# Moving one subtraction on the Vector engine: the low half of a head's first probability unit goes from ahead of row 7's maximum to behind the next head's first maxima

## The chip, the core and the metric

The kernel runs on one core of one Trainium2 chip. The metric is the device time of one execution in microseconds (us), lower is better. The engines are named as the profile names them: PE is TensorE (matmuls), DVE is VectorE, ACT is ScalarE, POOL is GpSimd, and SP is the engine whose queue issues the DMAs.

## The reference

A block of a transformer on x of shape 4 x 1024 x 512, in float32:

```
xn  = layernorm(x)
q, k, v = xn @ Wq.T, xn @ Wk.T, xn @ Wv.T          # 16 heads of 32 columns
scores  = q k^T / sqrt(32), causal mask
attn    = softmax(scores) @ v  -> @ Wo.T
gate    = silu((xn @ fp8(gate_w)) * gate_scale)
up      = (xn @ fp8(up_w)) * up_scale
ffn     = ((gate * up) @ fp8(down_w)) * down_scale   # inner width 1536
out     = x + attn + ffn
```

With 4 batches and 16 heads there are 64 attention heads of 1024 x 1024 scores each, and the feed-forward part works on 4096 rows.

## The kernel before

A first stage (up to about 285 us) normalises x, projects q, k and v, and prepares weights. Then `attend` runs 16 iterations of four heads (s = 0, 1, 2, 3; head n = 4 it + s). Each head is cut into nine steps (u = 0 to 8), so an iteration has 36 steps (k = 9 s + u). Between the attention work of the steps PE gets matmuls of the feed-forward part and, from iteration 4 on (`with_out`), of the output projection. Nothing is scheduled at run time: each engine has its own program, written out step by step with tables such as `LOW_STEP`, executes it in order, and waits on semaphores where it needs another's result.

A head's probabilities are made in two ways. The first six rows of 128 queries are made transposed, in six units of up to 512 columns: PE writes the scores of unit u (`scores`, L1453), ACT takes the exponential into one of five buffers p32 (`exponentials`, L1269), POOL zeroes the masked triangle (`select`, L1206), ACT copies the float16 high half (`take_high`, L1259), and DVE or POOL subtracts it to get the low half (`take_low`, L1060). DVE makes the low halves of units 0, 3 and 5, POOL those of 1, 2 and 4. Rows 6 and 7 of 128 queries are made untransposed: PE writes their scores into a pair of banks (`scores_of_row`, L1467, ending with the mask, L1471), DVE takes their maximum and turns it into a bias (`maximum_of_row`, L1395 and L1398), ACT takes the exponential (`exponentials_of_row`, L1276) and the high half (L1283), POOL the low half (`low_of_row`, L1212), and a transposing DMA (L1096) turns them for PE. The scores of unit 3 on PE wait until row 7's exponential has read its banks.

For the head two further on, PE and DVE find the maxima of the first six rows ahead of time: PE writes scores (`maxima_scores`, L209) into two banks in turn, DVE reduces them (`row_maxima`, L232, each followed by the read of its accumulator, or L237), eight such units numbered 0 to 7 in steps 4 to 8, and PE can fill a bank only when DVE has reduced the maxima two units earlier. PE turns the maxima of head n+1 (L262), DVE copies them (`copy_row`, L269), and SP stores them as a row into that head's q_st (`store_row`, L199), without which PE can't begin that head (L1453).

Further steps of DVE that matter here: `normalise` (L1352, L1353, L1358) ends a half of the head before; L1358 multiplies two SBUF tiles. `swiglu` (L1383, L1390) multiplies gate and up. In s = 0 and 1, `scale_down` (L1376) frees bank `misc` at u = 5; in s = 2 and 3, from iteration 4 on, `add_output` (L1367) frees it at u = 4 (k = 22 and 31). PE's turning of the maxima waits for whichever it is. On SP, in s = 3, the store of the output that L1367 makes (L1138) and a load of 512 KB of x (L1118) stand ahead of the next head's row (L199), and behind it the two transposes of the rows (L1096) and then the load of the next iteration's xn tile (L1084), which PE's first gate matmul (L1515) needs. POOL also makes the low halves of the fused feed-forward tile (L1194) and of the attention output (L1190), and adds the feed-forward result to x (L1186).

The order of DVE's steps within a head comes from `iteration` in the DVE block, L1401 to L1423:

```
if u == 4 and n > 0: normalise(n - 1, 0)
swiglu ...
if u in ROW_MAX_STEP: maximum_of_row(...)            # row 6 at u = 1, row 7 at u = 3
row_maxima(..., n + 2, ..., M_STEP.get(u, ()))       # u = 4: maxima units 0 and 1
for unit, head in of_head(LOW_STEP, n, u): take_low(...)
copy_row; normalise(n - 1, 1) at u = 8; add_output; scale_down
```

`LOW_STEP = {2: 0, 3: 1, 4: 2, 8: 3, 9: 4, 10: 5}` gives the step of each unit; 10 is step 1 of the next head. POOL uses the same table for its units.

Of the kernel before, what the change touches and what calls it, by code (L numbers as in the profile page):

```python
# [113 lines left out]

E_STEP = {0: 0, 1: 1, 2: 2, 6: 3, 7: 4, 8: 5}
HIGH_STEP = {1: 0, 2: 1, 3: 2, 7: 3, 8: 4, 9: 5}
LOW_STEP = {2: 0, 3: 1, 4: 2, 8: 3, 9: 4, 10: 5}
ROW_SCORES_STEP = {1: 0, 3: 1}
ROW_MAX_STEP = {1: 0, 3: 1}
# [44 lines left out]
def of_head(table, n, u):  # L164


    found = [(table[u], n)] if u in table else []
    if u + U in table and n > 0:
        found.append((table[u + U], n - 1))
    return found  # L170
# [787 lines left out]
def attend(nc, x, out, xn_dram, keep, rows, pair, bank):  # L958
# [5 lines left out]
    with ExitStack() as ctx:  # L964
# [88 lines left out]
        def take_low(eng, ops, units, u, n, signal):  # L1053

            if u not in units:
                return
            e, at = NE * n + u, slice(u * 512, u * 512 + UNIT_WIDTH[u])

            eng.wait_ge(p_hi, e + 1)
            ops.tensor_tensor(probs[n % 2][:, LO, at], p32[e % RING][:, 0:UNIT_WIDTH[u]], probs[n % 2][:, HI, at],  # L1060
                              ALU.subtract).then_inc(signal, 1)
# [111 lines left out]
        def _(pool):  # L1173
# [23 lines left out]
            def select(u, n):  # L1197

                if u not in DIAGONAL:
                    return  # L1200
                pool.wait_ge(exp_done, NE * n + u + 1)
                blocks = 2 if DIAGONAL[u] else 1
                step = DIAGONAL[u] or P
                at = p32[(NE * n + u) % RING][:, :].rearrange("p (b q) -> p b q", q=P)
                at = at[:, 0:(blocks - 1) * (step // P) + 1:step // P, :]
                nc.gpsimd.affine_select(out=at, in_=at, compare_op=ALU.is_ge, fill=0.0, base=0,  # L1206
                                        pattern=[[0, blocks], [1, P]], channel_multiplier=-1).then_inc(diag_done, 1)
# [7 lines left out]
            def iteration(it, with_out):  # L1215
                for s in range(HEADS_PER_IT):
                    n = 4 * it + s
                    for u in range(U):
                        k = s * U + u
                        if u in E_STEP:  # L1220
                            select(E_STEP[u], n)
                        for unit, head in of_head(LOW_STEP, n, u):
                            take_low(pool, nc.gpsimd, POOL_LOW, unit, head, p_lo_pool)
# [24 lines left out]
        def _(act):  # L1248
            def take_high(u, n):

                e, w = NE * n + u, UNIT_WIDTH[u]
                act.wait_ge(exp_done, e + 1)
                if u in DIAGONAL:

                    act.wait_ge(diag_done, ND * n + sorted(DIAGONAL).index(u) + 1)
                if u == 0:

                    wait(act, pv_mm, 2 * (n - 1))
                nc.scalar.copy(probs[n % 2][:, HI, u * 512:u * 512 + w], p32[e % RING][:, 0:w]).then_inc(p_hi, 1)  # L1259

            def exponentials(u, n):

                e, w = NE * n + u, UNIT_WIDTH[u]
                act.wait_ge(e_mm, e + 1)

                old = e - RING
                wait(act, p_lo_pool, low_parts(POOL_LOW, old))
                wait(act, p_lo_dve, low_parts(DVE_LOW, old))
                nc.scalar.activation(p32[e % RING][:, 0:w], st_bank[u % 2][:, 0:w],  # L1269
                                     ACT.Exp, scale=s_exp[:, :]).then_inc(exp_done, 1)  # L1270
# [29 lines left out]
            def iteration(it, with_out):  # L1300
                for s in range(HEADS_PER_IT):
                    n = HEADS_PER_IT * it + s
                    for u in range(U):
                        k = s * U + u
                        if u in E_STEP:
                            exponentials(E_STEP[u], n)
                        for unit, head in of_head(HIGH_STEP, n, u):
                            take_high(unit, head)
# [38 lines left out]
        def _(dve):  # L1347
# [53 lines left out]
            def iteration(it, with_out):  # L1401
                for s in range(HEADS_PER_IT):
                    n = 4 * it + s
                    for u in range(U):
                        k = s * U + u
                        if u == 4 and n > 0:
                            normalise(n - 1, 0)
                        for f, t in at_step(SWIGLU_STEP, it, k):
                            swiglu(f, t)
                        if u in ROW_MAX_STEP:  # L1410
                            maximum_of_row(ROW_MAX_STEP[u], n)
                        if n + 2 < NH:
                            row_maxima(nc, dve, rows, m_bank, n + 2, s % 2, M_STEP.get(u, ()))
                        for unit, head in of_head(LOW_STEP, n, u):
                            take_low(dve, nc.vector, DVE_LOW, unit, head, p_lo_dve)
                        if k in ROW_STEP and n + 1 < NH:
                            copy_row(nc, dve, rows, misc, n + 1, (s + 1) % 4, it if s == 0 else it + 1)
                        if u == U - 1 and n > 0:
                            normalise(n - 1, 1)
                        if with_out and k in ADD_OUT_STEP:  # L1420
                            add_output(ADD_OUT_STEP[k], it - LAG)
                        if k in ADD_DOWN_STEP and it > 0:
                            scale_down(ADD_DOWN_STEP[k], it - 1)  # L1423
# [271 lines left out]
```

## Time and profile before

| | before |
|---|---|
| median of 3 runs | 1320.91 us (1313.93 to 1323.89) |
| the profiled execution | 1318.2 us, of it span 1316.5 us |
| PE busy | 1240.5 us (94%) |
| DVE busy | 1074.4 us (82%) |
| ACT, POOL busy | 897.8 us (68%), 876.9 us (67%) |
| mean granted TensorE clock | 0.992 |
| DVE L1060 (low halves) | 192 instructions, 113.7 us, mean 605 ns |
| POOL L1212 (low halves of rows) | 128 instructions, mean 2017 ns |

Share of busy time alone does not say what bounds the kernel: PE's matmuls are pipelined and their ends are modelled, and the engines hand work to each other several times in each step. A wait is booked in brackets ahead of the instruction that waited ("[0.66 <-PE pair L1471]": the engine stood idle 0.66 us until PE's line 1471 wrote the pair of banks). An instruction of DVE or POOL can also be held up after it has started; then it has no bracket, and its own duration is longer than that of its equals.

### The profile page before, as it was taken

The numbers are of one execution on the slowest core, as the hardware profiler recorded it, in microseconds if no ns is written. First come the engines' busy times: TensorE is split into PE (matmuls) and PEld (weight loads), VectorE is DVE, ScalarE is ACT, GpSimd is POOL, SyncE is SP. The second block draws the span as 40 slices with busy tenths as digits, with TensorE's granted clock in tenths as the row PEclk, the third lists the DMA queues.
The fourth block names the chain that finished last, engine by engine and source line by source line (L and its number), as shares of the span: only waits on it lengthen the run. The fifth ranks groups of instructions, "written<-read, shape, count | busy, mean of one in ns | idle before, by whom it ended". The sixth has DMA issues, their size and how long they took to land.

```text
span 1316.5 us, 32425 instructions
## 1 busy us (share of the span) xinstructions
PE 1240.5 (94%) x11749; PEld 819.5 (62%) x11749; DVE 1074.4 (82%) x2615; ACT 897.8 (68%) x1527; POOL 876.9 (67%) x1017
## 2 busy tenths in 40 slices
PE   4999999987899898999999999999999999999988
PEld 3444444446666666677776767676767676776654
DVE  8888788868888888887988888888878787878862
ACT  4323323237777878788888888787878787878870
POOL 1332233127777777788887887877878787888882
PEclk9999999989999999999999999999999999999999
DMA  8699999834546464666666675767666556667555
GB/s 267 167 248 242 262 267 236 212 111 93 131 100 141 99 136 94 129 128 137 146 130 150 117 150 102 150 122 151 128 140 121 138 122 138 142 127 150 103 110 119
DMA packets 427599, 196.07 MB, mean 149 GB/s; under 512 B 339248, under 2 KB 396592, under 8 KB 427440
## 3 DMA queue, kind: packets, MB, share of 16 engines
q1 hardware_dynamic: 409024, 177.22, 60.4%
q10 hardware_dynamic: 18416, 16.78, 4.7%
q8 instruction: 94, 1.54, 0.5%
q14 instruction: 65, 0.53, 0.1%
HBM read 72.89 MB, written 42.21 MB: 87 GB/s over the span
## 4 chain that ended last, share of the span: by engine, by line
PE 45%; DVE 14%; issue 5%; DMA 5%; ACT 4%; POOL 3%; SPq 2%; ACTq 0%; DVEq 0%; POOLq 0%
PE bank L1515 14%; PE bank L1529 10%; PE bank L1491 7%; PE pair L1453 4%; PE pair L209 4%; DVE probs L1060 3%; DMA shared<-xn_parts 3%; PE bank L1537 2%; DVE row_top L1395 2%; DMA q_st<-m_row 2%; PE pair L1467 2%; DVE junk L232 2%; ACT probs L1259 2%; POOL row L1212 2%; DVE ga L1383 2%
## 5 line engine op out<-in xcount | busy, mean ns | idle before, releaser
L1269 ACT ACTIVATE p<-pair,s_exp 128x512 f32<-128x512 f32 (+1 forms) x384 | 243.6, 635 | 171.5 <-PE pair L1453 170.2
L1212 POOL TENSOR_TENSOR row<-row 128x896 f16<-128x896 f32 (+1 forms) x128 | 257.2, 2017 | 12.1 <-ACT row L1283 12.0
L1060 POOL TENSOR_TENSOR probs<-p,probs 128x512 f16<-128x512 f32 x192 | 223.0, 1165 | 0.2
L1259 ACT CAST probs<-p 128x512 f16<-128x512 f32 (+1 forms) x384 | 214.4, 558 | 10.8 <-POOL p L1206 9.0
L1515 PE MATMUL bank<-shared,wg 128*128 128x256 f16 x1536 | 201.9, 275 | 3.5 <-DMA shared<-xn_parts 3.5
L1515 PE MATMUL bank<-shared,wu 128*128 128x256 f16 x1536 | 202.4, 275 | 0.0
L1529 PE MATMUL bank<-wd,fuse 128*128 128x512 f16 x768 | 192.3, 381 | 0.8 <-DVE ff_out L1376 0.8
L1395 DVE TENSOR_REDUCE row_top<-pair 128x1 f32<-128x896 f32 (+1 forms) x128 | 147.6, 1153 | 44.3 <-PE pair L1471 44.3
L1206 POOL TENSOR_SCALAR_AFFINE_SELECT p<-p 128x128 f32<-128x128 f32 (+1 forms) x256 | 104.0, 411 | 118.2 <-ACT p L1269 117.6
L1194 POOL TENSOR_TENSOR fuse<-fu,fuse 128x512 f16<-128x512 f32 x96 | 120.7, 1257 | 62.5 <-ACT fuse L1298 62.3
L1515 PEld LDWEIGHTS bank<-shared,wg 128*128 128x128 f16 x1536 | 142.5, 98 | 29.7 <-DMA shared<-xn_parts 8.0
L1515 PEld LDWEIGHTS bank<-shared,wu 128*128 128x128 f16 x1536 | 143.6, 99 | 22.1 <-issue 0.2
L1276 ACT ACTIVATE row<-pair,row_bias,s_exp 128x896 f32<-128x896 f32 (+1 forms) x128 | 147.8, 1155 | 6.0 <-DVE row_bias L1398 6.0
L1453 PE MATMUL pair<-q_st,k_st 98*128 98x256 f16 (+3 forms) x640 | 136.8, 279 | 10.4 <-DMA q_st<-m_row 7.4
L1491 PE MATMUL bank<-v_sb,probs 128*128 128x65 f16 x2688 | 133.8, 192 | 8.1 <-DVE attn L1358 7.6
L1491 PEld LDWEIGHTS bank<-v_sb,probs 128*128 128x128 f16 x2688 | 118.7, 97 | 36.2 <-issue 15.8
L209 PE MATMUL pair<-k_st,q_st 96*128 96x128 f16 x504 | 125.4, 308 | 15.5 <-DVE mx L232 8.4
L232 DVE CUSTOM_DVE_ANT_0 junk<-pair,mask 128x128 bf16<-128x128 f32 x252 | 116.8, 482 | 24.1 <-PE pair L209 21.8
L1283 ACT CAST row<-row 128x896 f16<-128x896 f32 (+1 forms) x128 | 126.6, 989 | 0.0
L1060 DVE TENSOR_TENSOR probs<-p,probs 128x512 f16<-128x512 f32 (+1 forms) x192 | 113.7, 605 | 2.4 <-ACT probs L1259 2.4
L1383 DVE SCALAR_TENSOR_TENSOR ga<-th,bank 128x256 f32<-128x256 f32 x192 | 79.4, 413 | 34.2 <-ACT th L1290 32.5
L237 DVE TENSOR_REDUCE mx<-pair 128x1 f32<-128x512 f32 x128 | 87.8, 687 | 23.9 <-PE pair L209 23.9
(153 smaller groups left out, 2126.0 us busy)
## 6 DMA issues: line engine op xcount, KB each, us to landing
q_st<-q_parts SPq DMA_DIRECT2D x192, 64.0 KB, 2.6
k_st<-k_parts SPq DMA_DIRECT2D x192, 64.0 KB, 2.0
v_parts<-res SPq DMA_DIRECT2D x8, 1056.0 KB, 6.8
v_sb<-v_parts SPq DMA_DIRECT2D x64, 132.0 KB, 2.2
xn_parts<-x_t SPq DMA_DIRECT2D x16, 512.0 KB, 8.9
q_parts<-qk_st SPq DMA_DIRECT2D x32, 256.0 KB, 5.6
k_parts<-qk_st SPq DMA_DIRECT2D x32, 256.0 KB, 4.2
shared<-xn_parts SPq DMA_DIRECT2D x16, 512.0 KB, 4.9
```

Source lines behind the costliest of these rows:

```text
L209: nc.tensor.matmul(banks[u % len(banks)][:, 0:w], rows.q_st[i][part, blk * P:(blk + 1) * P], rows.k_st[i][part, k0:k0 + w], start=True, st ...
L232: ins = nc.vector.tensor_tensor_reduce(out=rows.junk[u % 2][:, 0:w], in0=src, in1=rows.mask[:, 512 - w:512], scale=1.0, scalar=at if k0 el ...
L1060: ops.tensor_tensor(probs[n % 2][:, LO, at], p32[e % RING][:, 0:UNIT_WIDTH[u]], probs[n % 2][:, HI, at], ALU.subtract).then_inc(signal, 1)
L1212: nc.gpsimd.tensor_tensor(row16[r][:, w:2 * w], row32[r][:, :], row16[r][:, 0:w], ALU.subtract).then_inc(row_lo, 1)
L1259: nc.scalar.copy(probs[n % 2][:, HI, u * 512:u * 512 + w], p32[e % RING][:, 0:w]).then_inc(p_hi, 1)
L1269: nc.scalar.activation(p32[e % RING][:, 0:w], st_bank[u % 2][:, 0:w], ACT.Exp, scale=s_exp[:, :]).then_inc(exp_done, 1)
L1276: nc.scalar.activation(row32[r][:, :], row_bank[r][:, 0:row_width(r)], ACT.Exp, bias=row_bias[:, r:r + 1], scale=s_exp[:, :]).then_inc(row ...
L1395: nc.vector.tensor_reduce(row_top[:, r:r + 1], row_bank[r][:, 0:row_width(r)], AX.X, ALU.max).then_inc(row_red, 1)
L1453: mm = nc.tensor.matmul(st_bank[u % 2][:, at:at + w], k_st[s][:, j * P:(j + 1) * P], q_st[s][:, q0:q0 + w], start=True, stop=True)
L1491: mm = nc.tensor.matmul(o_half[:, i % (QB // 2), :], probabilities(n, i, j, part), v_sb[s][:, j, 0:VN], start=(j == 0 and part == HI), sto ...
L1515: mm = nc.tensor.matmul(ff_bank[f % 2][:, h * FT:(h + 1) * FT], (wg8, wu8)[h][:, kc, f * P:(f + 1) * P], xt[:, part, kc, :], start=(part = ...
L1529: mm = nc.tensor.matmul(misc[:, :], fuse[:, part, f, i * P:(i + 1) * P], wd8[:, f, :], start=(f == 0 and part == HI), stop=(f == FC - 1 an ...
```

## The change

DVE gets a table of its own, in which unit 0 stands at step 4 and no longer at step 2. Units 3 and 5 stay, and POOL's steps stay.

```
+DVE_LOW_STEP = {4: 0, 8: 3, 10: 5}
 LOW_STEP = {2: 0, 3: 1, 4: 2, 8: 3, 9: 4, 10: 5}
...
                         if n + 2 < NH:
                             row_maxima(nc, dve, rows, m_bank, n + 2, s % 2, M_STEP.get(u, ()))
-                        for unit, head in of_head(LOW_STEP, n, u):
+                        for unit, head in of_head(DVE_LOW_STEP, n, u):
                             take_low(dve, nc.vector, DVE_LOW, unit, head, p_lo_dve)
```

So in each of the 64 heads one instruction of DVE, the subtraction of 128 x 512 elements for unit 0, moves from between `swiglu` of step 2 or 3 and row 7's maximum to behind maxima units 0 and 1 of step 4, ahead of `add_output` where there is one and of maxima unit 2 of step 5. No instruction and no wait is added or removed. The order of DVE's low halves among themselves stays 0, 3, 5.

## Rows read from the trace of the kernel before

**Rows 1.** The page, part 1: busy time of each engine.

```profile
PE 1240.5 (94%) x11749; PEld 819.5 (62%) x11749; DVE 1074.4 (82%) x2615; ACT 897.8 (68%) x1527; POOL 876.9 (67%) x1017
```

**Rows 2.** Chain that ended last, head 27 (s = 3): start, us, what.

```profile
711.67 0.68 DVE shared L1367
...
714.32 4.00 DMA q_st<-m_row
```

**Rows 3.** Timeline, head 27 (s = 3): start, us, engine, line, operation [idle before].

```profile
708.16 0.22 PE L1471 MATMUL pair<-mask_bf,ident_bf 128*128 128x128 bf16 x1
...
708.33 0.68 DVE L1060 TENSOR_TENSOR probs<-p,probs 128x512 f16<-128x512 f32 x1
708.93 1.22 DVE L1395 TENSOR_REDUCE row_top<-pair 128x1 f32<-128x1024 f32 x1
...
711.59 0.75 DVE L1367 SCALAR_TENSOR_TENSOR shared<-bank,c_out,res 128x512 f32<-128x512 f32 x1
...
711.01 1.17 POOL L1194 TENSOR_TENSOR fuse<-fu,fuse 128x512 f16<-128x512 f32 x1 [0.82 <-ACT fuse L1298]
```

**Rows 4.** Timeline, DVE and POOL on two SBUF inputs each, heads 10 and 27.

```profile
445.97 1.16 POOL L1060 TENSOR_TENSOR probs<-p,probs 128x512 f16<-128x512 f32 x1
...
446.39 1.28 DVE L1060 TENSOR_TENSOR probs<-p,probs 128x512 f16<-128x512 f32 x1
...
703.97 1.15 POOL L1060 TENSOR_TENSOR probs<-p,probs 128x512 f16<-128x512 f32 x1
...
704.03 1.24 DVE L1358 TENSOR_TENSOR attn<-o_sum,rsum 128x128 f32<-128x128 f32 x1
```

**Rows 5.** Timeline, POOL's L1194 in s = 3: heads 19 and 59.

```profile
588.98 1.16 POOL L1194 TENSOR_TENSOR fuse<-fu,fuse 128x512 f16<-128x512 f32 x1 [0.82 <-ACT fuse L1298]
...
1206.94 1.16 POOL L1194 TENSOR_TENSOR fuse<-fu,fuse 128x512 f16<-128x512 f32 x1 [0.91 <-ACT fuse L1298]
```

**Rows 6.** Timeline, head 25 (s = 1): POOL, DVE behind the maxima, PE.

```profile
679.28 1.95 POOL L1212 TENSOR_TENSOR row<-row 128x896 f16<-128x896 f32 x1
...
679.95 0.08 DVE L232 DVE_READ_ACCUMULATOR2_ANT mx<- 128x1 f32 x1
680.11 0.56 DVE L232 CUSTOM_DVE_ANT_0 junk<-pair,mask 128x384 bf16<-128x384 f32 x1
...
681.53 0.60 PE L209 MATMUL pair<-k_st,q_st 96*128 96x512 f16 x2
...
689.59 0.34 PE L1491 MATMUL bank<-v_sb,probs 128*128 128x65 f16 x6 [0.18 <-DVE attn L1358]
```

**Rows 7.** Timeline, POOL's L1212 of row 6 in s = 1: heads 5 and 61.

```profile
370.46 1.94 POOL L1212 TENSOR_TENSOR row<-row 128x896 f16<-128x896 f32 x1
...
1236.60 1.94 POOL L1212 TENSOR_TENSOR row<-row 128x896 f16<-128x896 f32 x1
```

**Rows 8.** Timeline, head 24 (s = 0): POOL, and DVE's wait at maxima unit 3.

```profile
662.79 2.33 POOL L1060 TENSOR_TENSOR probs<-p,probs 128x512 f16<-128x512 f32 x2
...
666.61 0.69 DVE L232 CUSTOM_DVE_ANT_0 junk<-pair,mask 128x512 bf16<-128x512 f32 x1 [0.64 <-PE pair L209]
```

**Rows 9.** Timeline, head 26 (s = 2): POOL's L1194.

```profile
695.71 1.17 POOL L1194 TENSOR_TENSOR fuse<-fu,fuse 128x512 f16<-128x512 f32 x1 [1.34 <-ACT fuse L1298]
```

**Rows 10.** Early iterations: PE in head 10 (timeline); chain at the end of head 7.

```profile
450.05 0.34 PE L209 MATMUL pair<-k_st,q_st 96*128 96x384 f16 x1 [1.36 <-DVE mx L232]
...
411.25 5.93 DMA shared<-xn_parts
```

**Rows 11.** Timeline, the store of the maxima's row and who needs it, heads 25 to 27.

```profile
683.25 0.20 DVE L269 COPY m_row<-bank 12x128 f16<-12x128 f16 x1
...
686.62 0.38 PE L1453 MATMUL pair<-q_st,k_st 98*128 98x512 f16 x1
...
700.52 0.65 SPq L199 DMA_DIRECT2D q_st<-m_row  x1
...
702.44 0.38 PE L1453 MATMUL pair<-q_st,k_st 98*128 98x512 f16 x1
```

More of the change, by code:

```diff
@@ L116 @@
 HIGH_STEP = {1: 0, 2: 1, 3: 2, 7: 3, 8: 4, 9: 5}
+DVE_LOW_STEP = {4: 0, 8: 3, 10: 5}
 LOW_STEP = {2: 0, 3: 1, 4: 2, 8: 3, 9: 4, 10: 5}
@@ L1413, in iteration @@
                             row_maxima(nc, dve, rows, m_bank, n + 2, s % 2, M_STEP.get(u, ()))
-                        for unit, head in of_head(LOW_STEP, n, u):
+                        for unit, head in of_head(DVE_LOW_STEP, n, u):
                             take_low(dve, nc.vector, DVE_LOW, unit, head, p_lo_dve)
```

## The prediction, as put on record before the changed kernel ran

> **What bounds the kernel now.** I read the page first: PE is busy 94% of the span [rows 1], but busy time of pipelined matmuls is no proof that PE is the bound. The chain of waits told more. Through heads s = 0 and 1 of an iteration it runs over PE alone. Through s = 2 and above all s = 3 it leaves PE: in s = 3 it runs over DVE's steps one behind the other up to `add_output`, then over SP (store of the output, load of x) and the small DMA of the next head's row [rows 2]. The next head can't begin before that DMA lands, so whatever delays `add_output` in s = 3 delays the whole kernel. Then I read the timelines of DVE, POOL and PE around the instruction that moves, head by head. From iteration 4 on the four heads of an iteration repeat to 0.01 us almost everywhere, so one head of each kind can stand for its kind.
>
> **What the instruction costs where it stands.** Alone it takes 0.68 us [rows 3]. In s = 0 and 1 DVE waits for PE's scores of row 7 behind it anyway, so it is free there. In s = 2 and 3 it isn't: in head 27 the scores of row 7 are there at 708.16 + 0.22 = 708.38, row 7's maximum starts at 708.93 [rows 3]. Without the low half in front it could start some 0.04 behind the scores, at 708.42, so 0.51 sooner. In iterations 0 to 3 the low half takes 1.28 instead of 0.68 [rows 4], and row 7's maximum could start about 1.20 sooner.
>
> **Why it took 1.28 us, and the price in the new place.** In head 10 POOL's subtraction runs from 445.97 to 447.13; DVE's, begun at 446.39, ends at 447.67, 0.54 behind POOL's end [rows 4]. In head 27 the short multiplication L1358 began 0.06 behind a POOL instruction and took 1.24, to 705.27, POOL's ended at 705.12 [rows 4]. So where POOL works on two SBUF tiles and DVE then starts an operation that does too, DVE's waits until POOL's ends, even if POOL was only 0.06 ahead. Maxima, `swiglu`, `scale_down` and `add_output` have an operand in PSUM, and aren't lengthened beside POOL. The price of the moved instruction is therefore: end of POOL's running instruction + 0.54 - its own start, at least 0.68. The next instruction of DVE starts about 0.08 before it ends.
>
> The Trainium skill, "SBUF — State Buffer", section "Who interferes with whom", states it as an exclusive lock: a DVE instruction with two SBUF inputs and a GpSimd instruction that reads SBUF block each other, whoever issues first holds the pair for the whole instruction. By that rule in its plain form the low half would end 0.68 behind POOL's end where the rows say 0.54; over the 27 heads priced below with a wait that is 27 x 0.14, some 4 us more than my sum, about 1339. It speaks against the change, which moves an instruction that was mostly clear of POOL next to POOL's longest ones.
>
> **Part by part.** *s = 3, from iteration 4 (heads 19, 23, ... 59: 11 heads).* Row 7's maximum, `normalise` and maxima 0 and 1 come 0.51 sooner. In their old place they end where `add_output` begins, 711.59, so the low half starts at 711.08. POOL's L1194 starts at 711.01, released by ACT, whose work there doesn't hang on row 7's maximum, and ends at 712.18 [rows 3]. The low half thus ends at 712.72, and `add_output` begins at 712.64: 1.05 later than before. L1194 stands in the same place in the first and the last of these heads [rows 5]. Behind `add_output` in the queues wait PE's turning of the maxima, SP's store, the load of x, the row, both transposes and the xn load; all are 1.05 later, and the chain passes through them [rows 2]. Nothing covers it. 11 x 1.05 = 11.5; head 59, whose scores come later, so that the 0.51 isn't won, 0.4 more.
>
> *s = 1 (16 heads).* DVE waits for PE before row 7's maximum, so nothing comes sooner. The low half would start at 679.95; POOL is in the low half of row 6 from 679.28 to 681.23 [rows 6], the same from head 5 to head 61 [rows 7]. It ends at 681.77. Maxima unit 2 starts at 681.69 and not at 680.11, and ends with its accumulator read at 682.26. PE needs it for maxima unit 4, the second of the two matmuls from 681.53, which started at about 681.75 [rows 6]: PE stops for 0.57. Up to here the chain is on PE, so this shows, less what PE waited anyhow at the next head's start, 0.18 for L1358 [rows 6]. L1358 itself waits for POOL, which follows PE: between 0.39 and 0.57, I take 0.48. 16 x 0.48 = 7.7.
>
> *s = 0 (16 heads).* POOL's two low halves end at 665.12 [rows 8], the moved one at 665.66, maxima unit 2 about 0.8 later than before. DVE stood 0.64 before unit 3 [rows 8], which takes up nearly all; PE asks for unit 2 only at 666.4. Nothing to 0.1; I take nothing.
>
> *s = 2, from iteration 4 (11 heads).* Again 0.51 sooner. L1194 starts at 695.71 [rows 9], 0.06 before the old start of `add_output` there, so the low half starts at 695.26, ahead of it: 0.68, no wait. `add_output` is 0.1 late, POOL is 0.1 to 0.2 late, and L1358 of the next head hangs on POOL. 11 x 0.1 = 1.1.
>
> *s = 2 and 3, iterations 0 to 3 (8 heads).* No `add_output` here. PE waited 1.36 for maxima unit 0 [rows 10]; that comes 1.20 sooner, and the low half behind it fits. In s = 2 that is won: 4 x 1.2 = 4.8. In s = 3 the next iteration waits for the xn tile [rows 10], whose load stands behind the transposes of POOL's row halves. These are no earlier, as POOL is held up by the low half. So s = 3 wins nothing (if the tile didn't bound, another 4.8). The last head has no maxima and wins about 1.
>
> Sum: 11.5 + 0.4 + 7.7 + 1.1 - 4.8 - 1.0 = 14.9. The sum is made against the profiled execution: 1318.2 + 14.9 = 1333.1. That execution lies 2.7 under the median of the runs, so in the median's terms 1335.8; I say 1335.
>
> **Rivals.**
> *A. DVE gets in ahead of POOL in s = 3.* POOL's lead there is 0.07 us. If the maxima run 0.1 us faster, the low half runs first, takes 0.68, and `add_output` is 0.1 late and not 1.05: 14.9 - 11 x 0.95 = +4.5, 1325. Against it: rows 4 show POOL winning with a lead of 0.06, and both sides repeat to 0.01. Chance 0.2.
> *B. Faster.* The low half doesn't collide in its new place and the freed time before row 7's maximum counts in full: 8 x 1.2 in early heads and 0.51 in each of 22 later ones, 9.6 + 11.2 = 20.8 off, 1300. It decides where `add_output` in s = 3 isn't what the next head waits for, or the low half lies in idle time of DVE. Against it: the low half stays ahead of `add_output`, so DVE's work up to it is the same even without POOL. Chance 0.07.
> *C. Slower still: the row of the maxima comes late in s = 1.* Its copy, behind maxima unit 4, moves from 683.25 to 684.83, PE needs it at 686.62 + 0.57 = 687.19 [rows 11]. Issued about 0.2 behind the copy, it would have 2.1; one issued at 700.52 served PE at 702.44 without a wait, 1.92 [rows 11]. But the one of s = 3 took 4.00 [rows 2]. Above 2.1 it decides: by 0.9 us in each of 12 heads +11, 1346.  Chance 0.13.
> *D. No effect:* the moved 0.68 are hidden in both places and all falls within 1321 +- 6. Chance 0.1.
>
> **How the numbers follow.** Forecast 0.5 (1328 to 1343). A measurement of this kernel can tell about 1% from no change, 13.2 us, so the border to slower is at 1334.1, inside the forecast: I give it 0.3 of 0.5 above and 0.2 below. With C slower has 0.43; A, D and the 0.2 make 0.5 within 1%; B 0.07. Range 1316 to 1346: it leaves out B and a little of D and C.
>
> **What the profile after would show.** Right: low halves of unit 0 of about 1.65 us in s = 3 and 1.8 in s = 1; `add_output` about 1.05 later in s = 3 against the scores of row 7; PE waiting about 0.6 for L232 at L209 in s = 1 and about 1 for L1367 at L262; DVE's busy sum up by some 30 us although it has the same instructions; in iterations 0 to 3 PE's wait at L209 of 1.36 gone. Wrong: a low half of 0.68 in s = 3 with L1194 lengthened (A), or a bracket for q_st<-m_row at the start of s = 2 (C).

## The result, and the profile after

The changed kernel takes 1341.5 us (median of 4 runs, 1340.0 to 1343.1) against 1321.2 us before: a ratio of 1.0169, with an interval of 1.0141 to 1.0197, so 20 us slower. Its profiled execution took 1343.1 us (span 1341.4), 24.9 more than the profiled one of before. One execution of one kernel below (the strided operation in the old place) took 3073.6 us, far from all the others, and is left out. All code behind L117 stands one line further down, so L1060 is now L1061, and so on.

Page, busy time of each engine, and the groups of low halves. Columns of a group: line, engine, operation, count, then busy us, mean ns of one, and idle time ahead of them.

```profile
PE 1246.0 (93%) x11748; PEld 818.0 (61%) x11749; DVE 1122.8 (84%) x2615; ACT 894.9 (67%) x1527; POOL 864.1 (64%) x1017
...
L1061 POOL TENSOR_TENSOR probs<-p,probs 128x512 f16<-128x512 f32 x192 | 230.3, 1202 | 0.5 <-ACT probs L1260 0.2
...
L1061 DVE TENSOR_TENSOR probs<-p,probs 128x512 f16<-128x512 f32 (+1 forms) x192 | 162.9, 849 | 2.0 <-ACT probs L1260 2.0
...
L1195 POOL TENSOR_TENSOR fuse<-fu,fuse 128x512 f16<-128x512 f32 x96 | 113.5, 1183 | 66.3 <-ACT fuse L1299 66.2
```

Against [rows 1], DVE is busy 48.4 us more with the same 2615 instructions. Its low halves are the main part: 113.7 us before, 162.9 now. The multiplication of `normalise` (L1358) adds 6.7 (77.0 to 83.7), and the rest became a little shorter. None of it is a wait in brackets; the instructions themselves became longer. POOL was busy 12.8 us less. The low half of DVE no longer stands beside two of POOL's operations. L1194 had a mean of 1257 ns before and has 1183 now. L255, the low half of the maxima, fell from 24.2 us to 12.9 for the same 64 instructions: in 21 of the heads of s = 2 and 3 from iteration 4 on it took 0.74 beside the low half, and takes 0.20 now. L1194 is the one that turned out to matter, in s = 0. L255 of head 27 before:

```profile
708.34 0.74 POOL L255 TENSOR_TENSOR m_part<-m_neg,m_part 128x6 f16<-128x6 f32 x1
```

PE's waits, after: who waited, for what, us in total, times, longest.

```profile
PE bank L263 <- DVE shared L1368: 15.1, 11, 1.4
...
PE pair L210 <- DVE mx L233: 12.3, 38, 0.4
...
PE pair L1454 <- DMA q_st<-m_row: 5.4, 10, 1.2
```

The first wait is new for the matmul: before, only the weight load that goes with it waited there, at most 0.27 us in 10 heads of s = 3. It has one case in each of the 11 heads of s = 3 from 19 to 59; head 63, the last, has no next head. The second, for the accumulators of the maxima, was 8.4 us in 7 cases (longest 1.4) and is now 12.3 in 38 short ones. The third was 7.4 in 10 (longest 1.5); it did not grow.

To see where the 24.9 us arise I took each head's first score matmul as its start. Before, heads 24, 25 and 28, with [rows 11] for 26 and 27 between them:

```profile
656.00 0.39 PE L1453 MATMUL pair<-q_st,k_st 98*128 98x512 f16 x1 [0.29 <-DMA q_st<-m_row]
...
671.32 0.38 PE L1453 MATMUL pair<-q_st,k_st 98*128 98x512 f16 x1
...
718.37 0.39 PE L1453 MATMUL pair<-q_st,k_st 98*128 98x512 f16 x1 [1.48 <-DMA q_st<-m_row]
```

After, heads 24 to 28:

```profile
660.59 0.38 PE L1454 MATMUL pair<-q_st,k_st 98*128 98x512 f16 x1
...
676.94 0.38 PE L1454 MATMUL pair<-q_st,k_st 98*128 98x512 f16 x1
...
692.85 0.38 PE L1454 MATMUL pair<-q_st,k_st 98*128 98x512 f16 x1
...
708.44 0.39 PE L1454 MATMUL pair<-q_st,k_st 98*128 98x512 f16 x1
...
724.11 0.39 PE L1454 MATMUL pair<-q_st,k_st 98*128 98x512 f16 x1
```

In this iteration the heads took 15.32, 15.30, 15.82 and 15.93 us before, and 16.35, 15.91, 15.59 and 15.67 after. Here s = 0 lost 1.03 and s = 1 lost 0.61. Summed over all iterations (after less before, us):

| | s = 0 | s = 1 | s = 2 | s = 3 |
|---|---|---|---|---|
| iterations 0 to 3 | +1.7 | +1.8 | -3.8 | -1.5 |
| from iteration 4 | +9.5 | +7.9 | -1.1 | +9.1 |
| predicted, all | 0 | +7.7 | -3.7 | +11.9 |

The eight sums make 23.6. The first stage, which the change does not touch, took 0.6 more in this execution, and what lies behind the start of the last head 0.7.

**Head 27 (s = 3), after:** timeline, start, us, engine, line, operation, idle before.

```profile
714.39 0.22 PE L1472 MATMUL pair<-mask_bf,ident_bf 128*128 128x128 bf16 x1
...
714.65 1.22 DVE L1396 TENSOR_REDUCE row_top<-pair 128x1 f32<-128x1024 f32 x1
...
717.24 1.16 POOL L1195 TENSOR_TENSOR fuse<-fu,fuse 128x512 f16<-128x512 f32 x1 [1.36 <-ACT fuse L1299]
...
717.32 1.63 DVE L1061 TENSOR_TENSOR probs<-p,probs 128x512 f16<-128x512 f32 x1
...
718.36 1.60 POOL L1061 TENSOR_TENSOR probs<-p,probs 128x512 f16<-128x512 f32 x1
718.87 0.74 DVE L1368 SCALAR_TENSOR_TENSOR shared<-bank,c_out,res 128x512 f32<-128x512 f32 x1
...
719.67 0.22 PE L263 MATMUL bank<-ident,m_part 128*12 128x128 f16 x1 [1.37 <-DVE shared L1368]
...
720.52 0.66 SPq L200 DMA_DIRECT2D q_st<-m_row  x1
```

From the end of the mask to `add_output` it was 3.21 us before [rows 3] and is 4.26 now, 718.87 - 714.61: 1.05 later. L1195 starts 0.08 ahead of the low half, which then takes 1.63 and ends 0.55 behind it. POOL's next low half then takes 1.60 where its equals take 1.16: it started while DVE's was still at work. So when both have instructions queued, they take turns. The Trainium skill, "SBUF — State Buffer", "Who interferes with whom", says that whoever issues first holds the shared port pair for the whole instruction and the other blocks fully; the two lengthened instructions here agree with that. By its plain form the low half would end 0.68 behind L1195, and the trace has 0.55. So the 1339 that the prediction worked out from that form is nearer to the measured time, but what its own sum lacks is the loss in s = 0, not those 0.14 us.

What follows `add_output` is delayed in two ways. PE now waits 1.37 at its turning of the maxima. On SP the row's store came only 0.20 later, seen from the head's start (720.52 - 708.44 = 12.08, and 714.32 - 702.44 = 11.88 before), where `add_output` came 1.28 later (10.43 and 9.15), because the issue of the load of x ahead of it had been long before. Its row before, then after:

```profile
712.77 1.50 SPq L1118 DMA_DIRECT2D res<-in_L_attn_x  x1
```

```profile
720.04 0.43 SPq L1119 DMA_DIRECT2D res<-in_L_attn_x  x1
```

**Head 25 (s = 1), after:** the same columns.

```profile
684.90 1.94 POOL L1213 TENSOR_TENSOR row<-row 128x896 f16<-128x896 f32 x1
...
685.57 1.82 DVE L1061 TENSOR_TENSOR probs<-p,probs 128x512 f16<-128x512 f32 x1
687.31 0.54 DVE L233 CUSTOM_DVE_ANT_0 junk<-pair,mask 128x384 bf16<-128x384 f32 x1
...
687.92 0.39 PE L210 MATMUL pair<-k_st,q_st 96*128 96x512 f16 x1 [0.39 <-DVE mx L233]
```

The low half ends 0.55 behind POOL's L1213, and maxima unit 2 is late for PE. That matmul, unit 4's, stands 10.98 behind the head's start and not 10.43, 0.55 later. Of this 0.39 is booked as a wait.

**Head 24 (s = 0):** three rows of before, then those of after.

```profile
660.27 1.71 POOL L1194 TENSOR_TENSOR fuse<-fu,fuse 128x512 f16<-128x512 f32 x1 [0.72 <-ACT fuse L1298]
...
661.63 1.22 DVE L1395 TENSOR_REDUCE row_top<-pair 128x1 f32<-128x1024 f32 x1 [0.67 <-PE pair L1471]
...
663.53 0.57 DVE L1358 TENSOR_TENSOR attn<-o_sum,rsum 128x128 f32<-128x128 f32 x1
```

```profile
664.84 1.16 POOL L1195 TENSOR_TENSOR fuse<-fu,fuse 128x512 f16<-128x512 f32 x1 [0.72 <-ACT fuse L1299]
...
666.20 1.23 DVE L1396 TENSOR_REDUCE row_top<-pair 128x1 f32<-128x1024 f32 x1 [1.26 <-PE pair L1472]
...
666.82 2.27 POOL L1061 TENSOR_TENSOR probs<-p,probs 128x512 f16<-128x512 f32 x2
668.11 1.13 DVE L1359 TENSOR_TENSOR attn<-o_sum,rsum 128x128 f32<-128x128 f32 x1
...
669.05 1.93 POOL L1213 TENSOR_TENSOR row<-row 128x896 f16<-128x896 f32 x1
...
669.71 1.81 DVE L1061 TENSOR_TENSOR probs<-p,probs 128x512 f16<-128x512 f32 x1
...
672.06 0.39 PE L210 MATMUL pair<-k_st,q_st 96*128 96x512 f16 x1 [0.39 <-DVE mx L233]
```

Here the forecast was "nothing". Before, the low half stood beside POOL's L1194 and lengthened it to 1.71. With the low half gone L1195 takes 1.16, and POOL is about 0.55 further on: its two low halves, which stood 1.16 behind the start of row 7's maximum (662.79 [rows 8] against 661.63), now stand 0.62 behind it (666.82 against 666.20). Two collisions follow. L1358 used to start at 663.53, before the end of POOL's first low half (662.79 + 2.33 / 2 = 663.96), got in ahead of the second and took 0.57. Now the second, which begins at about 666.82 + 2.27 / 2 = 667.96, is 0.15 ahead of it, and it takes 1.13. And when the moved low half comes, POOL has already begun its 1.93 us low half of row 6, and DVE's takes 1.81. Both maxima 0 and 2 are late for PE. Seen from the head's start, PE's turning of the maxima (L262, now L263) stood 11.15 behind it before and stands 12.22 behind it after, 1.07 later.

### The profile page after: what moved, and what is told of

It reads as the page before. It is cut to its first block, busy times and chain, and to the rows that moved or that the text cites. A ratio compares the mean times of both kernels' runs of the same rounds, so it can differ in the third digit from the quotient of the medians.

```text
span 1341.4 us, 32424 instructions
## 1 busy us (share of the span) xinstructions
PE 1246.0 (93%) x11748; PEld 818.0 (61%) x11749; DVE 1122.8 (84%) x2615; ACT 894.9 (67%) x1527; POOL 864.1 (64%) x1017
## 4 chain that ended last, share of the span: by engine, by line
PE 41%; DVE 17%; issue 10%; DMA 4%; ACT 3%; POOL 2%; SPq 1%; ACTq 0%; DVEq 0%; POOLq 0%
PE bank L1516 13%; PE bank L1530 8%; PE bank L1492 6%; DVE row_top L1396 5%; DVE junk L233 4%; PE pair L1454 4%; PE pair L210 3%; PE pair L1468 3%; PE bank L1538 2%; DMA q_st<-m_row 2%; DVE probs L1061 2%; DMA shared<-xn_parts 2%; PE pair L1538 2%; DVE o_sum L1354 1%; ACT probs L1260 1%
## 5 line engine op out<-in xcount | busy, mean ns | idle before, releaser
L1213 POOL TENSOR_TENSOR row<-row 128x896 f16<-128x896 f32 (+1 forms) x128 | 258.4, 2025 | 4.8 <-ACT row L1284 3.2
L1061 POOL TENSOR_TENSOR probs<-p,probs 128x512 f16<-128x512 f32 x192 | 230.3, 1202 | 0.5 <-ACT probs L1260 0.2
L1207 POOL TENSOR_SCALAR_AFFINE_SELECT p<-p 128x128 f32<-128x128 f32 (+1 forms) x256 | 96.7, 380 | 126.0 <-ACT p L1270 124.4
L1061 DVE TENSOR_TENSOR probs<-p,probs 128x512 f16<-128x512 f32 (+1 forms) x192 | 162.9, 849 | 2.0 <-ACT probs L1260 2.0
L1516 PEld LDWEIGHTS bank<-shared,wg 128*128 128x128 f16 x1536 | 142.2, 98 | 33.5 <-DMA shared<-xn_parts 11.9
L1195 POOL TENSOR_TENSOR fuse<-fu,fuse 128x512 f16<-128x512 f32 x96 | 113.5, 1183 | 66.3 <-ACT fuse L1299 66.2
L210 PE MATMUL pair<-k_st,q_st 96*128 96x128 f16 x504 | 130.3, 309 | 19.6 <-DVE mx L233 12.3
L1530 PEld LDWEIGHTS bank<-wd,fuse 128*128 128x128 f16 x768 | 68.8, 98 | 61.3 <-issue 2.7
```

The source lines that it names most:

```text
L210: nc.tensor.matmul(banks[u % len(banks)][:, 0:w], rows.q_st[i][part, blk * P:(blk + 1) * P], rows.k_st[i][part, k0:k0 + w], start=True, st ...
L1213: nc.gpsimd.tensor_tensor(row16[r][:, w:2 * w], row32[r][:, :], row16[r][:, 0:w], ALU.subtract).then_inc(row_lo, 1)
L1516: mm = nc.tensor.matmul(ff_bank[f % 2][:, h * FT:(h + 1) * FT], (wg8, wu8)[h][:, kc, f * P:(f + 1) * P], xt[:, part, kc, :], start=(part = ...
L1530: mm = nc.tensor.matmul(misc[:, :], fuse[:, part, f, i * P:(i + 1) * P], wd8[:, f, :], start=(f == 0 and part == HI), stop=(f == FC - 1 an ...
```

## The experiments

The twelve kernels are made from the changed one (the one with step 3 from the kernel of before, with the table shown there). Ratios are against the kernel of before, run on the same chip with them: its medians were 1316.6, 1318.1 and 1317.8 us in the three groups.

**The change in one kind of head at a time.** The two tables are chosen by s:

```
-                        for unit, head in of_head(DVE_LOW_STEP, n, u):
+                        for unit, head in of_head(DVE_LOW_STEP if s == 0 else LOW_STEP, n, u):
```

and likewise with s == 1, s == 2 and s == 3.

> The move is made in heads s = 0 alone (16 of 64), elsewhere unit 0's low half stays in front of row 7's maximum. Port theory (DVE's subtraction waits until POOL's running instruction on SBUF ends): the changed kernel's trace shows heads s = 0 longer by 1.04 us from iteration 4 on, and unit 0's low half of 1.81 us there; so +10 to +12 us here (15 heads, fewer in iterations whose xn tile is late anyway), 1332. Rival 'order alone' (the 0.68 us of work only stand in the way of what follows on DVE, POOL is no part of it): DVE had 0.64 us of idle time behind them in s = 0, so 0 to +1, 1321. Rival 'spread' (the loss has no place of its own, it comes of clock or DMA): a quarter of it, +5.

> The move in heads s = 1 alone. Port theory: the low half of unit 0 waits for POOL's 1.95 us low half of row 6 and takes 1.8 us, PE stops before maxima unit 4; 16 heads x 0.61 = +9.8 us, 1330. 'Order alone': the third maximum of step 5 would end at about 681.1 of the trace before and PE asks for it at 681.75, so 0, 1321. 'Spread': +5.

> The move in heads s = 3 alone. Port theory: add_output is 1.05 us later in 11 heads from iteration 4 on, as the low half starts 0.07 behind POOL's L1195 and takes 1.63; +11.5, less 1 to 3 us that heads 3, 7, 11 and 15 win: +9 to +11, 1331. 'Order alone': row 7's maximum comes 0.51 sooner and add_output 0.1 later, so +1 - 3 = -2, 1319. 'Spread': +5.

> The move in heads s = 2 alone. Port theory: the low half starts ahead of POOL's L1195 from iteration 4 on and takes 0.68 to 0.69, early it takes 1.11; the changed kernel's trace gives -3.8 for the four early heads and -0.3 in most later ones, so -4 to -7, 1311. A loss here would say that the move costs something even where POOL is not in the way.

| moved in | median | ratio, interval | difference |
|---|---|---|---|
| s = 0 | 1327.3 | 1.0083 (1.0068 to 1.0098) | +10.7 |
| s = 1 | 1325.3 | 1.0066 (1.0053 to 1.0079) | +8.8 |
| s = 3 | 1327.4 | 1.0082 (1.0064 to 1.0100) | +10.8 |
| s = 2 | 1315.5 | 0.9981 (0.9968 to 0.9993) | -2.6 |

The sum of the four is 27.7, the whole change 20.3 by the medians and 24.9 by the profiled executions. The interval of the whole is 19 to 26 us and each of the four is uncertain by about 2, so most of the gap can be noise. The loss is not one event with a long tail: s = 0, 1 and 3 carry about a third each. The move in s = 2 alone gained 2.6 where 4 to 7 were expected: its four early heads gave 3.7 by the profile, and the late heads gave part of it back. The move in s = 0 costs 10.7 by itself. The heads of s = 0 are 9.3 us longer in it from iteration 4 on, and the rows are those of the whole change. (In the same execution the late heads of s = 3, where nothing was moved, are 5.3 shorter, and those of s = 2 are 2.1 longer. A sum by kind of head is therefore worth less than the time of the whole kernel.) Timeline of that kernel, head 24:

```profile
666.89 1.18 DVE L1359 TENSOR_TENSOR attn<-o_sum,rsum 128x128 f32<-128x128 f32 x1
...
667.88 1.93 POOL L1213 TENSOR_TENSOR row<-row 128x896 f16<-128x896 f32 x1
...
668.54 1.82 DVE L1061 TENSOR_TENSOR probs<-p,probs 128x512 f16<-128x512 f32 x1
```

With the move in s = 3 alone, the heads of s = 3 are 6.4 longer from iteration 4 on and the heads behind them, s = 0, 3.5: part of the delay shows only there. PE waits for the xn tile, which SP loads behind the rows, 7.7 us in 12 cases, and 3.5 in 6 before.

**Is it POOL's head start that makes s = 0 lose?** The move in s = 0 alone, and POOL gets one more instruction, a memset of an unused tile, behind its low half of the fused tile. It gives back what the move has taken from POOL.

```
+        pause = sb("pause", [P, 512], BF16)
...
+                        if k == 1 and it > 0:
+                            nc.gpsimd.memset(pause[:, :], 0.0)
```

> As the move in s = 0 alone, and POOL gets one instruction more: it writes zeros to a spare tile of 128 x 512 bfloat16 behind its L1195 (now L1196) in step 1 of every iteration but the first. It tests why s = 0 loses 1.04 us: POOL is 0.54 us earlier there, since the low half no longer stands beside L1195, so POOL's second low half starts ahead of the multiplication L1359 and holds it 0.56 longer, and POOL's low half of row 6 starts ahead of the moved one. If so, an added 0.4 to 0.8 us of work on POOL puts both back: L1359 0.57 and not 1.13, the moved one about 1.1 and not 1.81, and nearly all of the 10.7 us goes: 0 to +3 against the kernel before. If POOL's time has no part in it, the loss stays, +10 or more. If the write takes much over 0.8 us it delays POOL itself and tells less.

Measured: 1317.7 us, 1.0002 (0.9986 to 1.0017). With fifteen more instructions on POOL the loss of 10.7 is gone. POOL's own row over the execution (count, then min, median and max in ns), and the timeline of head 24:

```profile
L1233 POOL MEMSET pause<- x15: 517/522/529, 351.5 to 1219.0; 128x512 bf16 x15
```

```profile
662.73 0.52 POOL L1233 MEMSET pause<- 128x512 bf16 x1
...
664.07 2.33 POOL L1062 TENSOR_TENSOR probs<-p,probs 128x512 f16<-128x512 f32 x2
...
664.89 0.49 DVE L1362 TENSOR_TENSOR attn<-o_sum,rsum 128x128 f32<-128x128 f32 x1
...
665.85 1.09 DVE L1062 TENSOR_TENSOR probs<-p,probs 128x512 f16<-128x512 f32 x1
...
666.36 2.34 POOL L1214 TENSOR_TENSOR row<-row 128x896 f16<-128x896 f32 x1
```

The normalisation's multiplication (here L1362) takes 0.49 (0.57 before, when it also got in between POOL's two), and the low half 1.09: it waits only for the rest of POOL's second one and then goes first, so that POOL's row half is the one lengthened (2.34 and not 1.93). DVE's order of work is that of the kernel that moves s = 0 alone. What differs is when POOL is where. That refutes, for s = 0, that the order of DVE's own steps costs the time: a low half of 1.09 us in the new place costs nothing there, one of 1.82 together with a multiplication of 1.18 costs 10.7.

**The move where only the freed time counts.** In iterations 0 to 3 there is no `add_output`. The move is made there alone, in s = 2 and 3.

```
+                        for unit, head in of_head(DVE_LOW_STEP if it < LAG and s > 1 else LOW_STEP, n, u):
```

> The move in s = 2 and 3 of iterations 0 to 3 alone (8 of 64 heads), where the low half of unit 0 took 1.28 us in its old place. Port theory: the low half in front of row 7's maximum waits for POOL there, so 1.2 us are won in each of heads 2, 6, 10 and 14; the heads s = 3 win only as far as the xn tile's load allows. The changed kernel's trace gives -3.8 for the s = 2 heads and -1.5 for the s = 3 heads, so -5 (-7 to -4), 1316, faster than both kernels. 'Order alone': 0.68 x 4 at the most, -2.7. 'Spread': 0 to +3.

Measured: 1312.5 us, 0.9970 (0.9959 to 0.9982), 4.1 us faster than before, and the fastest of these kernels. From the profile the heads of s = 2 in iterations 0 to 3 took 5.0 us less and those of s = 3 1.4 less. PE's wait for the maxima fell from 8.4 us (7 cases, longest 1.4) to 1.4 us (7 cases, longest 0.3). The moved low half of head 10 met POOL's L1195 and took 1.10 us (timeline), yet the head was 1.2 us shorter, as no `add_output` stands behind it:

```profile
445.35 1.10 DVE L1061 TENSOR_TENSOR probs<-p,probs 128x512 f16<-128x512 f32 x1
```

**One input in place of two.** To have the order of the changed kernel without the collision, I replaced the subtraction of unit 0 by an operation with one SBUF input (it multiplies by 0, so unit 0's low half is left out of the result), once in the old place and once in the new.

```
+            if u == 0:
+                ops.tensor_scalar(probs[n % 2][:, LO, at], p32[e % RING][:, 0:UNIT_WIDTH[u]], 0.0, None, ALU.mult
+                                  ).then_inc(signal, 1)
+                return
```

> Old place, but DVE's instruction for unit 0 has one SBUF input and not two: it multiplies the 128 x 512 exponentials by 0 in place of subtracting the high half from them, so the low half of unit 0 is left out of the result (zero). It serves as the base of the next run. Port theory: it no longer waits for POOL, nor POOL for it; so the 1.28 us of the early heads s = 2 and 3 become at most 0.68, worth up to 0.6 us in 4 to 8 heads, and where it hindered POOL's L1195 in s = 0 POOL runs 0.54 earlier, which alone makes L1359 collide (+0.3 a head in s = 0): -3 to +4 us against the kernel before.

> New place in all heads, again with the multiplication by 0 of one SBUF input for unit 0 (its low half is left out). Port theory: the instruction takes the same time as in the old place in every head (0.68 or less, no 1.63 and no 1.81), and the 20 us of the change go: against the run with one input in the old place -5 to +3. If the instruction form takes POOL's port too, its durations in the new place will be long again and say so. 'Order alone': what the instruction reads makes no difference, +15 to +22 against the old place.

Measured: 0.9981 (0.9967 to 0.9995) in the old place, 1.0100 (1.0080 to 1.0121) in the new. This was no control. All 64 instructions, with min, median and max in ns, old place and new:

```profile
L1062 DVE TENSOR_SCALAR probs<-p x64: 416/419/1386, 290.5 to 1265.0; 128x512 f16<-128x512 f32 x64
```

```profile
L1062 DVE TENSOR_SCALAR probs<-p x64: 419/1367/1557, 292.7 to 1276.6; 128x512 f16<-128x512 f32 x64
```

The operation takes 0.42 alone, but beside POOL it took up to 1.56, 1.14 more. So an operation with one SBUF input can be held up in the same way. The Trainium skill, "SBUF — State Buffer", "Who interferes with whom", says so of `tensor_scalar` where it runs in a two-port mode; the trace agrees in the lengthening, and shows no mode.

Then the same with every second element on both operands, which I hoped would leave that mode:

```
+                ops.tensor_scalar(probs[n % 2][:, LO, at].rearrange("p (b a) -> p a b", a=2),
+                                  p32[e % RING][:, 0:UNIT_WIDTH[u]].rearrange("p (b a) -> p a b", a=2), 0.0, None, ALU.mult
```

> Old place, unit 0's subtraction on DVE replaced by a multiplication by 0 of the exponentials alone, every second element first (so the low half of unit 0 is left out, zero). The one before, on contiguous elements, took 0.42 us alone and was itself lengthened beside POOL (up to 1.56 in the new place), so it was no control. This form reads and writes with a stride of two elements. Port theory, if this form doesn't take what POOL uses: about 0.68 us (the duration of the subtraction alone) in every head, also in the early s = 2 and 3 where the subtraction took 1.28. Against the kernel before -4 to +2.

> The same strided multiplication by 0 (low half of unit 0 left out) in the new place of all heads. Port theory: its duration is about 0.68 in all heads though POOL works beside it, and of the change's 20 to 25 us nearly all goes; what is left is that POOL runs earlier in s = 0 than before and L1359 collides: against strided_old -6 to +3. 'Order alone': the same amount of DVE work stands in the same new place, so +15 to +22 against strided_old. If the durations are long in spite of one input and a stride, the form contends and the run doesn't tell.

Measured: 0.9989 (0.9975 to 1.0003) and 1.0086 (1.0070 to 1.0103). The new place:

```profile
L1062 DVE TENSOR_SCALAR probs<-p x64: 451/1394/1594, 292.6 to 1281.4; 128x512 f16<-128x512 f32 x64
```

Neither slower alone nor free of POOL: again no control. What the pairs do show is that an instruction that alone is 0.26 or 0.23 us shorter than the subtraction still costs 13 to 14 us when it is moved there (1329.65 - 1315.74, 1329.79 - 1316.32). A control that has the subtraction's length and does not meet POOL was not had.

The pair on contiguous elements tells something else, because the collided instruction ends 0.28 behind POOL's and not 0.55. PE's wait for `add_output` at its turning of the maxima is shorter by just this:

```profile
PE bank L263 <- DVE shared L1372: 12.2, 11, 1.1
```

It is 1.10 in each of the 11 heads, against 1.37 in the changed kernel. In the old place there is none. In s = 1 the late heads are 0.37 us longer each with it (4.4 in 12), against 0.66 with the subtraction (7.9 in 12). So the end of the collided instruction is passed on one for one in both places. Without a collision the end of the subtraction would lie 1.14 us sooner in s = 1 (1.82 - 0.68), which is more than these heads lose, and 0.95 sooner in s = 3 (1.63 - 0.68), most of PE's 1.37. That last step is worked out, not measured. The nearest measurement is s = 2 from iteration 4 on. There `add_output` stands behind the moved low half too, which takes 0.69 without a wait, and these heads changed by only -1.1 together in the changed kernel.

**Step 3 in place of step 4.** If the price is the end of POOL's running instruction + 0.54 - the own start, it can be worked out for another place.

```
-DVE_LOW_STEP = {4: 0, 8: 3, 10: 5}
+DVE_LOW_STEP = {3: 0, 8: 3, 10: 5}
```

> Unit 0's low half at step 3 in all heads, directly behind row 7's maximum and its bias and ahead of the normalisation. Port theory, with the price end of POOL's running instruction + 0.54 - own start: in s = 1 it starts at 678.3 of the trace before, beside POOL's second low half (to 679.33), and takes 1.5; the normalisation and maxima 0 and 1 come 1.5 later, and PE waits for maxima unit 0: +0.9 to 1.2 in each of 31 heads s = 0 and 1; in s = 3 it meets POOL between two instructions, so add_output 0.1 late and not 1.05; early s = 2 and 3 won as in the change, -5. Together +20 to +30, 1345, with the loss in s = 0 and 1 alone. 'Order alone': 0.68 us ahead of maxima unit 0, about +0.3 in these 31 heads, +10, less 5.

Measured: 1368.8 us, 1.038 (1.036 to 1.040), 51 slower. Timeline, head 25 (s = 1):

```profile
695.31 2.32 POOL L1061 TENSOR_TENSOR probs<-p,probs 128x512 f16<-128x512 f32 x2
...
696.62 1.55 DVE L1061 TENSOR_TENSOR probs<-p,probs 128x512 f16<-128x512 f32 x1
697.59 2.33 POOL L1213 TENSOR_TENSOR row<-row 128x896 f16<-128x896 f32 x1
...
698.61 1.45 DVE L1359 TENSOR_TENSOR attn<-o_sum,rsum 128x128 f32<-128x128 f32 x1
...
700.33 0.34 PE L210 MATMUL pair<-k_st,q_st 96*128 96x384 f16 x1 [2.12 <-DVE mx L233]
```

The low half itself came out as priced, 697.63 + 0.54 - 696.62 = 1.55. The loss is about twice the 20 to 30 that were expected. What I had not seen is the second collision: the low half is late, so L1359 no longer comes between POOL's instructions but 1 us into the 2.33 us row half, and takes 1.45. PE then waits 2.12. The heads of s = 1 from iteration 4 on are 31.6 us longer together, 2.6 each; in s = 2 and 3, where the low half took 0.68 in this place, they changed by nearly nothing, also in iterations 0 to 3, where 5 less were expected. The late heads of s = 0 are 9.5 longer and the early ones of s = 1 7.9. The whole of PE's waits for the maxima is 44.8 us in 30 cases. The place one step earlier more than doubles the loss.

**Behind `add_output`.** In s = 2 and 3 unit 0's low half goes behind `add_output`; in s = 0 and 1 it stays in its old place.

```
+                            if s > 1 and unit == 0:
+                                continue
...
+                        if s > 1 and u == 4:
+                            take_low(dve, nc.vector, DVE_LOW, 0, n, p_lo_dve)
```

> Heads s = 0 and 1 as before; in s = 2 and 3 unit 0's low half stands at step 4 behind add_output. Port theory: in the early iterations the same gain as in the run with the move there alone (-4 to -6); from iteration 4 on add_output in s = 3 comes 0.51 sooner and the low half, which waits for POOL's L1195 all the same, is behind it and no more on the way to the next head's row. But maxima unit 2 is 0.4 late and PE waits for it, up to 0.7. So per late iteration between -0.5 and +0.2: -5 to -11 together, 1309, faster than both kernels and perhaps than the early move alone. 'Order alone': the same sign, -6 to -12.

Measured: 1318.2 us, 1.0005 (0.9995 to 1.0014): no change, where 5 to 11 less were expected. The loss of s = 3 is gone (its heads from iteration 4 on are 4.0 us shorter together, and those of s = 2 in iterations 0 to 3 5.0). But the late heads of s = 2 are 4.2 longer and those of s = 0 4.5. Maxima unit 2 now stands behind `add_output` and the low half, and PE waits for the maxima 10.2 us in 26 cases: 0.40 in each late head of s = 2 and 0.47 in each of s = 3. In s = 0 it does not wait for them more than before. There it waits for the xn tile, 7.3 us in 10 cases against 3.5 in 6, so s = 0 gives back what s = 3 won.

## Why the prediction held, and where it didn't

The forecast was 1335 with a range of 1316 to 1346, and 14.9 more than before; 1341.5 is in the range, 20 to 25 more. The mechanism was right in s = 1 and 3: DVE's low half meets POOL and is held up by it. One step failed, s = 0, and several terms were off in size. That the time still lies inside the range is owed to its width. Without s = 0 the profiles differ by 13.6 (24.9 - 11.3), close to the 14.9, but that is luck in part: s = 1 came out 2.0 higher than its term and s = 3 and the late heads of s = 2 5.0 lower.

- **The price rule held.** For s = 3 it gave 1.64 and 1.63 was measured; for s = 1 1.82, and 1.82; in step 3 of s = 1 1.5 and 1.55. Operations with an operand in PSUM stay as they were, as assumed: `scale_down`, L1377, took 678 to 692 ns in all 32 cases after the change.
- **s = 3, late heads.** Predicted 11.5 + 0.4, `add_output` later by 1.05. It was later by just 1.05, and PE waits for it in 11 heads (15.1 us). The heads' lengths grew by 9.1: the term was right in mechanism and 2.8 too large. What it had left out is that the issues ahead of the row on SP don't always take as long. Head 27, which stood for all, is even 0.26 shorter (15.67 for 15.93). There SP took 1.50 us before to issue the load of x, and 0.43 after. So the row was issued only 0.20 later, seen from the head's start, and PE, which had waited 1.48 for it at the start of head 28, now starts that head 3.59 behind the issue with no wait. Before, three of the 11 heads had such a long issue (0.98 in head 23, 1.50 in 27, 1.35 in 43; 0.39 to 0.43 in the others); after, none. These three changed by +0.25, -0.26 and +0.04, the other eight by 9.1 together, 1.14 each. Why that issue is long at times is open. In the kernel with s = 3 alone a part (3.5) came out one head later.
- **s = 1.** Predicted 16 x 0.48 = 7.7, measured 9.7, of them 7.9 in the 12 late heads. A usual late head lost 0.61. PE's stop of 0.57 was right (0.55 measured, 0.39 of it in brackets); what I took off for the wait of 0.18 at the next head's start [rows 6] was wrong: the head lost more than PE's stop, not less.
- **s = 0: "Nothing to 0.1; I take nothing".** This is the step that failed: 11.3 us in the whole change (9.5 late) and 10.7 when it is done alone. I used POOL's times of before [rows 8] for the new kernel, though the instruction I moved had itself been lengthening POOL's L1194, from 1.16 to 1.71. Without that POOL comes 0.55 sooner, and the two instructions that had just missed it meet it. The kernel with the memset shows that this shift is the cause: 0.52 us more of work on POOL takes the loss back to nothing. The same was overlooked in s = 2 and 3, where the move frees POOL's L255 of 0.54 us; no loss was traced to that.
- **s = 2, late heads.** Predicted +1.1, measured -1.1. The low half went ahead of L1194 and took 0.69, as said. The 0.51 that was freed before row 7's maximum was worth a little more than the 0.1 that I charged for `add_output`. With s = 2 alone the same heads made +1.0, so even the sign of this small term depends on the neighbours. s = 1 and 2 together, late, were predicted at 0.58 per iteration and measured at 0.57, but only because the two misses cancel.
- **Iterations 0 to 3.** Predicted -4.8 in s = 2; -3.8 in the whole change, -3.7 with s = 2 alone and -5.0 in the kernel that moves nothing else. In s = 3 the 1.5 won are given back in s = 0 (+1.7), where the next iteration waits for its xn tile, as was said. But moving s = 0 alone gives +1.9 there too, so in the whole change the two causes don't add up.
- **The last head.** Predicted -1.0; what lies behind its start took 0.7 more.
- **The rivals.** A (DVE first in s = 3): the low half took 1.63 and not 0.68. C (the maxima's row late in s = 1) hardly showed: PE waited for that DMA at the start of s = 2 in two heads, 0.7 us together, where C had 0.9 in each of 12. B is refuted by the sum, but its reasoning was right where there is no `add_output`: the fastest kernel is just that part of the change.
- **Of the signals named**, PE's waits were 0.39 for the maxima in s = 1 (about 0.6 said) and 1.37 for `add_output` (about 1 said), and the early waits of 1.36 are gone. DVE's busy sum was to go up by some 30 us and went up by 48. Most of the 18 more are the low halves of s = 0 (15 of 16 took 1.81, where the ends that I worked out allowed about 1.1) and the multiplications L1358 beside them (6.7). That signal points at the failed step.

Two things stay open. That the collision costs the time in s = 1 and 3 is not shown by a kernel without it. It rests on the durations of the low half, on who waits behind it, and on PE's waits, which are 0.27 shorter where the instruction ends 0.27 sooner. And the four parts sum to 27.7 while the whole is 20 to 25: noise covers most of this, and delays in neighbouring heads may cover each other.

## What to carry to other kernels

Before moving an instruction between two engines that hold each other up, price both ends: where it goes it waits for the other engine, and where it leaves it gives time back to that engine, whose next instructions then come sooner and can meet others that had just missed them. So redo the other engine's timeline first, and only then read off the collisions. And apply such a move only in the stages whose chain runs over the freed place: here the move in 8 heads of 64 gained 4 us (the four of s = 2 carry it), and the same move in all of them lost 20. And before one head stands for its kind, compare each wait and issue that the sum rests on over all heads: the one that stood for s = 3 here was one of three with a long issue on SP.

## What the runs showed of the hardware that I had not expected

- An operation of DVE with one SBUF input (128x512, float32 to float16, `tensor_scalar`) takes 0.42 us alone and up to 1.56 beside POOL; with every second element 0.45, and up to 1.59. Counting inputs in SBUF, as I did in the prediction, is not enough to say that an operation is free of POOL.
- When both engines have instructions queued they take turns: DVE's gets in at POOL's next boundary, and POOL's next is held up in its turn (1.60 for 1.16 in head 27, 2.34 for 1.93 in the kernel with the memset). A lead of 0.08 us was enough for POOL to go first (head 27 after). Where both started within 0.01 us, as POOL's L255 and DVE's low half did in head 27 before, it was POOL's that became longer, 0.74 for 0.20, while DVE's took its 0.68.
- More work on an engine can make a kernel faster than the same kernel without it: 15 memsets of 0.52 us took the ratio from 1.0083 to 1.0002.
- Issuing the same load of 512 KB on SP took 0.43 us in most heads and 0.98 to 1.50 in three (23, 27 and 43 before).
